# Late new-value products and split convolutions in a three-direction recurrent kernel

## The reference, cut to what matters

```python
gi = x @ wih.T ; gh = h @ whh.T            # three gates of 128 channels each
r = sigmoid(ir + hr) ; z = sigmoid(iz + hz)
n = tanh(i_n + r * h_n)
out = (1 - z) * n + z * h                  # the context, an output of the step
h = tanh(conv1d(out, cw) + cb)             # three taps along the line, 128 by 128 channels each
```

## Time and profile before

| | us |
|---|---|
| median of 3 runs | 370.1 (367.79 to 370.64) |
| the profiled execution | 367.54 |
| its span, first to last instruction | 365.8 |
| TensorE products, busy | 330.9 (90%) |
| VectorE busy | 309.7 (85%) |
| ScalarE busy | 277.8 (76%) |
| mean granted TensorE clock | 0.989 of full |

### The profile page before, as it was taken

The page is one execution under the profiler, slowest core; times in us unless marked ns, Lnnn a source line. Parts: engine busy times, 40 slices in busy tenths (PEclk is TensorE's granted clock), DMA queues, the critical chain, the costliest instruction groups (busy, mean ns, idle before and its releaser), DMA issues.

```text
span 365.8 us, 7776 instructions
## 1 busy us (share of the span) xinstructions
PE 330.9 (90%) x2720; PEld 260.7 (71%) x2720; DVE 309.7 (85%) x772; ACT 277.8 (76%) x590; POOL 4.2 (1%) x16
## 2 busy tenths in 40 slices
PE   1574758999998999999999999999999999999995
PEld 0233646778787888888888888888888888873442
DVE  2965778999997999889999999999998988887875
ACT  3977867888887888888888888888888888867400
POOL 2010000000000000000000000000000000000000
PEclk9988999999999999999999999999999999999999
DMA  8900000000000019100000000000000000000433
GB/s 301 372 1 2 2 0 2 0 2 3 0 3 0 2 26 398 39 0 0 0 0 0 0 0 0 0 0 0 0 0 0 0 0 0 0 0 34 174 139 115
DMA packets 5343, 14.75 MB, mean 40 GB/s; under 512 B 720, under 2 KB 848, under 8 KB 5328
## 3 DMA queue, kind: packets, MB, share of 16 engines
q1 hardware_dynamic: 5328, 14.55, 10.4%
HBM read 10.36 MB, written 4.19 MB: 40 GB/s over the span
## 4 chain that ended last, share of the span: by engine, by line
PE 75%; ACT 12%; issue 6%; DVE 5%; POOL 1%; POOLq 0%; ACTq 0%
PE rz_bank L765 19%; PE conv_bank L765 16%; PE rz_bank L768 9%; PE n_bank L765 9%; PE conv_bank L768 8%; PE n_bank L768 4%; ACT rz L440 3%; ACT x_col L435 2%; ACT x_rows L412 2%; DVE x_rows L571 1%; ACT hval L457 1%; ACT ctx_store L463 1%; PE rz_bank L851 1%; ACT nval L452 1%; DVE npre L657 1%
## 5 line engine op out<-in xcount | busy, mean ns | idle before, releaser
L765 PE MATMUL conv_bank<-ctx_store,w_parts 128*128 (+1 forms) x558 | 110.0, 277 | 6.5 <-ACT ctx_store L463 4.6
L765 PE MATMUL rz_bank<-h_parts,w_parts 128*128 128x256 f16 x372 | 76.1, 273 | 0.0
L440 ACT ACTIVATE rz<-rz_bank,descale 128x512 f32<-128x512 f32 x96 | 65.9, 687 | 10.4 <-PE rz_bank L765 5.6
L765 PEld LDWEIGHTS conv_bank<-ctx_store,w_parts 128*128 128x128 f16 x558 | 53.9, 98 | 25.2 <-ACT ctx_store L463 12.4
L452 ACT ACTIVATE nval<-npre 128x256 f32<-128x256 f32 x93 | 38.5, 413 | 41.5 <-DVE npre L669 41.5
L657 DVE SCALAR_TENSOR_TENSOR npre<-n_bank,descale,rz 128x256 f32<-128x256 f32 x93 | 44.9, 483 | 27.4 <-ACT rz L440 26.2
L768 PE MATMUL conv_bank<-ctx_store,w_parts 128*128 (+1 forms) x279 | 67.7, 276 | 0.0
L765 PE MATMUL rz_bank<-x_rows,w_parts 128*128 (+1 forms) x256 | 52.9, 274 | 4.5 <-DVE x_rows L571 4.5
L457 ACT ACTIVATE hval<-conv_bank,biases,descale 128x256 f32<-128x256 f32 x93 | 52.0, 560 | 3.1 <-PE conv_bank L765 3.0
L768 PE MATMUL rz_bank<-h_parts,w_parts 128*128 128x256 f16 x186 | 45.7, 273 | 0.0
L765 PE MATMUL n_bank<-h_parts,w_parts 128*128 128x256 f16 x186 | 45.7, 273 | 0.0
(11 more groups left out here) (118 smaller groups left out, 499.9 us busy)
## 6 DMA issues: line engine op xcount, KB each, us to landing
x<-x_dram SPq DMA_DIRECT2D x16, 512.0 KB, 7.8
out_dram<-x_rows SPq DMA_DIRECT2D x16, 256.0 KB, 2.0
ctx_store<-weights_dram SPq DMA_DIRECT2D x3, 576.0 KB, 11.7
ctx_store<-weights_dram SPq DMA_DIRECT2D x1, 192.0 KB, 12.6
biases<-biases_dram SPq DMA_DIRECT2D x1, 2.0 KB, 12.3
```

What stands on the lines that cost most here:

```text
L440: nc.scalar.activation(rz[k][:].rearrange("p g c -> p (g c)"), rz_bank[k][:], ACT.Sigmoid, scale=gate_scale(k)).then_inc(sig_done[k], 1)
L765: last = nc.tensor.matmul(out, w_block(HI, k, n), parts(hi_or_lo), start=start, stop=stop and hi_or_lo == LO, skip_group_check=True)
```

## The change: what it does

- **New-value products late.** The hidden part of the new value is written to the first half of `n_bank` (`hidden_new`, three products). `reset_hidden` multiplies it by the reset gate in place in PSUM. The three input products are then added onto it (`new_products`), in the block of `now`. `tanh_argument` is gone: the tanh reads PSUM with its scale in every step.
- **Convolutions in two parts.** `convolution_hi` (six products of the high context half) runs one block after the context, the first three of them ahead of `new_products` and three behind. `convolution_lo` (three products) runs in the next block, between the hidden gate products and `hidden_new`.
- **High context half on VectorE** (`context_hi`, now a one-source instruction), right behind `blend`. ScalarE's hidden tanh moves behind the sigmoid and the splits.
- **Head.** The strip of the last columns is two wide and is split before the first sigmoid, as are the weights "in 2"; the column piece between it and the next strip is split in block (1, 1). TensorE waits for the strip at block (0, 0). The six last warming products are gone.
- **Block (31, 2).** The first chunk parts are ahead of all else in it; the chunk parts after the blocks stand behind the late new-value products of the last step.

The diff, cut to its core:

```diff
-FRONT_WARM, CHAIN_WARM, LAST_WARM = 12, 4, 6
+FRONT_WARM, CHAIN_WARM = 12, 4
+CONV_AHEAD = 3
-LAST_COLS = Cells((2, H - 2), (W - 4, W))
+LAST_COLS = Cells((2, H - 2), (W - 2, W))
...
-    (0, 0): LAST_COLS,
-    (1, 0): Cells((2, 4), (0, W - 4)),
-    (1, 1): Cells((H - 4, H - 2), (0, W - 4)),
+    (1, 0): (Cells((2, 4), (0, W - 2)),),
+    (1, 1): (Cells((H - 4, H - 2), (0, W - 2)), Cells((4, H - 4), (W - 4, W - 2))),
...
-WAIT_SPLITS = ((0, 0), (1, 2), (2, 0), (3, 2), (4, 0), (7, 2), (8, 0), (10, 1))
+WAIT_SPLITS = ((0, 0), (0, 1), (1, 2), (2, 0), (3, 2), (4, 0), (7, 2), (8, 0), (10, 1))
...
@@ scalar
             weights_hi(UNITS.index("in 1"))
+            weights_hi(UNITS.index("in 2"))
+            x_hi(LAST_COLS, 2)
...
             def new_value(k, s):
-                if is_first(s):
...
-                else:
-                    act.wait_ge(npre_done[k], s)
-                    nc.scalar.activation(nval[k][:], npre[k][:], ACT.Tanh).then_inc(n_done[k], 1)
+                act.wait_ge(n_full[k], s + 1)
+                nc.scalar.activation(nval[k][:], n_bank[k][:, 0:COLS], ACT.Tanh,
+                                     scale=gate_scale(k)).then_inc(n_done[k], 1)
...
             def steps(t, j):
...
-                if exists(before[1], STEPS - 2) and not starting:
-                    hidden(*before)
                 if exists(nxt[1]):
                     gates(*nxt)
...
-                if exists(now[1]):
-                    context_hi(*now)
                 if exists(before[1], STEPS - 2):
-                    if starting:
-                        hidden(*before)
+                    hidden(*before)
                     hidden_hi(*before)
@@ vector
             weights_lo(UNITS.index("in 1"))
+            weights_lo(UNITS.index("in 2"))
+            x_lo(LAST_COLS)
...
             def reset_hidden(k, s):
                 dve.wait_ge(sig_done[k], s + 1)
-                dve.wait_ge(n_ready[k], s + 1)
-                nc.vector.scalar_tensor_tensor(npre[k][:], n_bank[k][:, COLS:2 * COLS], gate_scale(k),
-                                               rz[k][:, 0, :], ALU.mult, ALU.mult).then_inc(rh_done[k], 1)
+                dve.wait_ge(n_ready[k], s)
+                nc.vector.tensor_tensor(out=n_bank[k][:, 0:COLS], in0=n_bank[k][:, 0:COLS],
+                                        in1=rz[k][:, 0, :], op=ALU.mult).then_inc(rh_done[k], 1)
+
+            def context_hi(k, s):
+                dve.wait_ge(ctx_done[k], s + 1)
+                nc.vector.tensor_scalar(context_lines(k, s, HI), context[k][:].rearrange("p b l -> p (b l)"),
+                                        ACT_SCALE, None, ALU.mult).then_inc(ctx_hi_done[k], 1)
...
-            def tanh_argument(k, s):
...
             def steps(t, j):
...
                     blend(*now)
+                    context_hi(*now)
                 if exists(nxt[1]) and not is_first(nxt[1]):
                     reset_hidden(*nxt)
...
-                    tanh_argument(*nxt)
...
@@ tensor
-            warm(LAST_WARM)
...
+            def new_products(k, s):
+                first = is_first(s)
+                def x_parts(part):
+                    return x_line(k, s, part)
+                ahead(pe, s, x_parts(HI), x_parts(LO))
+                if not first:
+                    pe.wait_ge(rh_done[k], s)
+                passes(n_bank[k][:, 0:COLS], k, 2, x_parts, HI, start=first)
+                passes(n_bank[k][:, 0:COLS], k, 2, x_parts, LO, stop=True).then_inc(n_full[k], 1)
...
+            def hidden_new(k, s):
+                pe.wait_ge(n_done[k], s)
+                passes(n_bank[k][:, 0:COLS], k, GATES + 2, parts, HI, start=True)
+                passes(n_bank[k][:, 0:COLS], k, GATES + 2, parts, LO, stop=True) \
+                    .then_inc(n_ready[k], 1)
...
+            CONV_HI = [(tap, part) for tap in range(TAPS) for part in (HI, LO)]
+            def convolution_hi(k, s, first, end):
+                if first == 0:
+                    ahead(pe, s + 1, *(tap_lines(k, s, HI, tap) for tap in range(TAPS)))
+                    pe.wait_ge(ctx_hi_done[k], s + 1)
+                    if k == 2:
+                        pe.wait_ge(h_done[0], s + 1)
+                    elif not is_first(s):
+                        pe.wait_ge(h_done[1 if k == 1 else 2], s)
+                for tap, part in CONV_HI[first:end]:
+                    nc.tensor.matmul(out, w_block(part, k, 2 * GATES + tap), tap_lines(k, s, HI, tap), ...)
+            def convolution_lo(k, s):
+                ahead(pe, s + 1, *(tap_lines(k, s, LO, tap) for tap in range(TAPS)))
+                pe.wait_ge(ctx_lo_done[k], s + 1)
+                ...                                # three products, then conv_ready
...
             def steps(t, j):
+                # order: (chunk parts at (31, 2)), hidden_gates(now), convolution_lo(two back),
+                # hidden_new(now), wait for splits, input_gates(nxt), convolution_hi(one back, 0..3),
+                # new_products(now), convolution_hi(one back, 3..6)
...
-            pe.wait_ge(npre_done[1], STEPS - 1)
+            pe.wait_ge(n_done[1], STEPS)
             for c in (2, 3):
                 chunk_part(c, 0)
```

More of the change, by code:

```diff
@@ L472, in steps @@
                 now, nxt, before = lagged(t, j, 0), lagged(t, j, -1), lagged(t, j, 1)
[L474 removed]
                 if exists(now[1]):
[L476 removed]
+                    ahead(act, now[1], now[1] + 1)
                     new_value(*now)
[L478 to L479 removed]
                 if exists(nxt[1]):
@@ L816, in hidden_products, with tap_lines @@
                     .then_inc(n_ready[k], 1)
-            def convolution(k, s):
+            def tap_lines(k, s, part, tap):
+                return ctx_store[k][:, part, line(k, s), :, tap:tap + LINE]
+            CONV_HI = [(tap, part) for tap in range(TAPS) for part in (HI, LO)]
+            def convolution_hi(k, s, first, end):
                 out = conv_bank[k % 2][:, 0:COLS].rearrange("p (b l) -> p b l", b=B)
-                def tap_lines(part, tap):
-                    return ctx_store[k][:, part, line(k, s), :, tap:tap + LINE]
-                ahead(pe, s + 1, *(tap_lines(part, tap) for part in (HI, LO) for tap in range(TAPS)))
-                pe.wait_ge(ctx_hi_done[k], s + 1)
-                if k == 2:
-                    pe.wait_ge(h_done[0], s + 1)
-                elif not is_first(s):
-                    pe.wait_ge(h_done[1 if k == 1 else 2], s)
-                for part in (HI, LO):
-                    if part == LO:
-                        pe.wait_ge(ctx_lo_done[k], s + 1)
-                    for tap in range(TAPS):
-                        last = passes(out, k, 2 * GATES + tap,
-                                      lambda p: tap_lines(p, tap), part,
-                                      start=part == HI and tap == 0, stop=tap == TAPS - 1)
@@ new lines, in convolution_hi @@
+                if first == 0:
[6 more added lines that the diff above has]
+                for tap, part in CONV_HI[first:end]:
+                    nc.tensor.matmul(out, w_block(part, k, 2 * GATES + tap), tap_lines(k, s, HI, tap),
+                                     start=(tap, part) == (0, HI), stop=False, skip_group_check=True)
@@ new lines, in convolution_lo @@
+            def convolution_lo(k, s):
+                out = conv_bank[k % 2][:, 0:COLS].rearrange("p (b l) -> p b l", b=B)
+                ahead(pe, s + 1, *(tap_lines(k, s, LO, tap) for tap in range(TAPS)))
+                pe.wait_ge(ctx_lo_done[k], s + 1)
+                for tap in range(TAPS):
+                    last = nc.tensor.matmul(out, w_block(HI, k, 2 * GATES + tap), tap_lines(k, s, LO, tap),
+                                            start=False, stop=tap == TAPS - 1, skip_group_check=True)
@@ L873, in steps @@
             def steps(t, j):
-                k, s = lagged(t, j, 2)
-                if isinstance(s, int) and s == 0:
-                    pe.wait_ge(w_lo_done, UNITS.index(f"conv {k}") + 1)
-                if exists(s, STEPS - 2):
-                    convolution(k, s)
-                if j == 2 and isinstance(t, int) and t == STEPS - 1:
+                now, nxt, last, before = (lagged(t, j, lag) for lag in (0, -1, 1, 2))
+                if isinstance(t, int) and (t, j) == (STEPS - 1, 2):
                     pe.wait_ge(w_lo_done, len(UNITS))
-                    pe.wait_ge(npre_done[0], STEPS - 1)
+                    pe.wait_ge(n_done[0], STEPS)
                     pe.wait_ge(ctx_lo_done[0], STEPS)
```

127 lines of the change are left out of this document (60 added, 67 removed).

## The result

| | before | after |
|---|---|---|
| median, 9 runs each | 370.35 us (367.79 to 370.64) | 374.31 us (371.8 to 374.68) |
| the profiled execution | 367.54 | 373.17 |
| its span | 365.8 | 371.1 |

The changed kernel takes 1.011 times as long, interval 1.0077 to 1.0143. It is slower by about 4 us; 372.0 was forecast, with a range of 366.5 to 379. The runs of both kernels fall in two groups some 2.5 us apart (before three at 367.8 to 368.3 and six at 370.1 to 370.6, after two at 371.8 and 371.9 and seven at 373.2 to 374.7), and the profiled execution before (367.54) is like its lower ones, the one after like its upper ones.

The account below looks back on a forecast made before the run. The prediction took TensorE's own list of 27 products a block (2.96 us) to bound the loop from step 11; 2.6 + 0.8 - 1.4 + 1.3 = +3.3 gave 370.8 or 373.4, forecast 372 us, range 366.5 to 379.

Parts of the forecast that it names:

- Settled loop: From step 11 on: convolution 0.16 and reset 0.07 late behind the column copy, step 9.10 instead of 8.97, +2.6 us.
- Rival 1: Block behind the column copy: context high takes 0.44, step loses 0.37 rather than 0.23, time 376; chance 0.2.
- main case: Whole kernel: the prediction's own case, sum +3.3 us, from -1 to +5; chance 0.5.
- Opening: First blocks: products wait for the narrow strip, run at half clock, and the second tanh comes later; +0.8 us.
- split blocks: Steps 1 to 10: low split and low context leave the loop, the wait moves to the bank; -1.4 us.
- range for the clock: Opening: ends of its +0.8 us term, -1.2 (clock never low) and +1.5.
- End: After the last step: three late products behind sigmoid and reset stand ahead of eighteen output products; +1.3 us.
- sum +3.3: Whole kernel: the four terms added, 370.8 us from the profiled execution or 373.4 from the median.
- Rival 2: Split blocks fall to PE's floor if the bank wait is nothing: -7.4 instead of -1.4, time 366; chance 0.2.
- Rival 3: Looped part: address work on PE's queue shows at 0.05 to 0.1 us a block, time 377; chance 0.05.
- Rival 4: Whole kernel: nothing moves, PE's list being as long; only the end's +1.3 us; chance 0.05.

Follow-up runs that it names:

- e3: The changed kernel with the context's high half in a two-source form, at 442 instead of 302 ns; median 377.09 us, ratio to before 1.0229.
- e10: The changed kernel with direction 2's convolution in its own slot and the column copy in two halves; median 362.38 us, ratio to before 0.9817.
- e2: The changed kernel with twelve useless products in TensorE's 2.8 us wait ahead of block (1, 1)'s first convolution; median 372.63 us, ratio to before 1.0086.
- e9: The changed kernel with direction 2's convolution in the free half of its new-value bank, column copy whole; median 370.03 us, ratio to before 1.0022.
- e11: The changed kernel's loop with the head of the kernel before, six last warming products included; median 373.34 us, ratio to before 1.0119.
- e12: e10 with six chunk products moved ahead of the last late products in block (31, 2); median 362.07 us, ratio to before 0.981.
- e1: The changed kernel with the six last warming products put back; median 373.74 us, ratio to before 1.010.
- e8: The kernel before with only its column copy cut in two halves around the new-value tanh; median 366.56 us, ratio to before 0.9941.
- e6: The changed kernel with hidden tanh and hidden high half ahead of ScalarE's splits in the first blocks; median 385.92 us, ratio to before 1.0436.
- e7: The kernel before with the rebuilt head and nothing of the loop's rework; median 371.4 us, ratio to before 1.0037.

## Why the prediction was right, and where a step failed

- **Settled loop, +2.6, measured +2.5.** Step 9.092 against 9.10. Context high took 302 ns (taken 300), tanh out of PSUM 469 (461), reset in place 430 (taken 480, lower end 420). The chain copy, tanh, blend, context half, convolution was named link by link, and e3 shows it: the longer context half moved the step by its own length. That the sum came out so close is in part luck. It was 8.87 for the list plus 0.16 for the convolution and 0.07 for the reset; the runs have 8.903 for the list (e10) and 0.19 above it, all of it at the convolution, with no wait for the reset. The Trainium skill, "VectorE: DVE Perf Modes", section "Mode 2×_2P", has this one-source form take two elements a cycle, and the two-source form can't; 302 ns against 442 for the same 272 elements agrees.
- **What that step left out.** A second wait ends at the same place 0.09 earlier, the hidden tanh that frees the bank. The prediction had put that tanh at 1.44 to 2.00 of the block and never asked which convolution it releases there. In the settled loop it changed nothing in the forecast, and everything in what the cure is.
- **Rival 1, context half at 0.44.** Its price was 3.9 us over the main case; made so (e3), the ratio goes from 1.011 to 1.0229, some 4.4 us, and 28 steps at 0.143 make 4.0. The price of the mechanism was right and its condition was not met.
- **Opening and split blocks, +0.8 and -1.4, measured +1.4 together.** This is the term that was mis-sized, by 2.0 us in the profiled executions, and two misses partly cancel in it. The opening, up to the copy of step 1, came out at 0.0 (42.51 against 42.52) rather than +0.8, which is within the spread of the head. The split blocks, from there to the copy of step 11, came out at +1.4 rather than -1.4: step 1 to 2 lost 1.94, and steps 2 to 11 gained 0.54 (87.60 against 88.14). The prediction saw that the bank would take the place of the context half as the wait, and still gave these blocks a gain. Of the 1.94, 1.2 is the second fall of the clock (e2); of the rest, either the bank's wait away (e9, step 13.59) or the old head (e11, 13.56) takes nearly all. In steps 2 to 11 the bank's wait cost another 1.9: without it they take 85.69 (e9), a gain of 2.4 on the kernel before. The prediction's range for the clock, -1.2 to +1.5, was about the first fall only.
- **End, +1.3, measured +1.4.** Six of the eighteen products can be put into the pause, for 1.1 in the trace (e12).
- **From one execution to the median.** The sum +3.3 was set against a low profiled run, and the forecast put between its two answers (370.8 and 373.4). The second was the better one: the medians differ by 4.0, and 1.4 of the 2.3 us by which 372 missed comes from this choice. It bears on the term above too. In every trace with this loop and whole copies the settled step is 9.09 (but for e3's longer context half), and in four of them (the change, e1, e2, e11) steps 2 to 11 take 87.6, so what sets one execution apart from the next seems to lie ahead of the copy of step 2. An estimate from the medians, 4.0 less 2.5 and 1.4, leaves about +0.1 for opening and split blocks in a middling execution, not the +1.4 of the pair that was profiled; against the forecast -0.6 the miss is then 0.7.
- **Rival 2** (split blocks at the floor, 366) fails on the bank, as its condition said. With the bank's wait and the whole copy away the split blocks do give 4.9 of its 7.4 (e10 against e8). **Rival 3** (address work) is refuted by e10. **Rival 4**, the end's +1.3 alone, is refuted by the step.

## What to carry to other kernels

When an instruction is moved behind others on its queue, ask not only who reads its result but who waits for the buffer that it frees; here the hidden tanh did both, and its second role cost 1.9 us in steps 2 to 11 and hid what the change gains. Where two waits end within 0.1 us of each other at one place, removing either alone measures as nothing, which does not show that either is harmless: remove both. And a reordering on one engine has to be followed through the queues of those that work with it, as the 11.6 us of e6 show. Last, one profiled execution a kernel can come from either end of its spread: compare stretches that repeat between traces, and check the sum against the medians.

## What was not expected of the hardware

- **Whether the clock falls after a pause was not the pause's length alone.** It fell after TensorE's waits of 2.84 us (the changed kernel) and 2.52 (e7), and stayed at 1.00 after 2.99 (e3), 2.80 (e11) and 2.48 (before), all in the same step. One kernel may do both in different executions: with the longer context half three runs were at 376.0 to 376.7 and a mean clock of 0.982, three at 377.5 to 378.9 and 0.977, but only one of the first was profiled. The clock can't be the whole of such a gap: the kernel before has one of the same size, with mean clocks of 0.984 to 0.989 in its shorter runs and 0.981 to 0.986 in its longer ones. What decides either stays open. TensorE's order of time in the run with the longest of these waits, and its busy time by stretch right behind:

```profile
48.56 0.49 PE L834 MATMUL conv_bank<-ctx_store,w_parts 128*128 128x256 f16 x3 [2.99 <-ACT hval L453]
```

```profile
49.00:50.00 1.00, 1.00 (x12) 0.89 (x10) 0.75 (x3) 0.47 (x1) 0.00 (x0) 1.00 0.00 0
```

- **Full clock right ahead of the first products did not carry over.** In e1 six wide products ran from 23.72 at full clock; the granted clock was 0.90 in the microsecond in which they ended and 0.50 from 25 to 37 us, where narrower products and pauses follow.
- **The VectorE instruction that reads and writes PSUM in place** took 430 ns for 256 columns, beside 425 for one in SBUF and 483 for the form of the earlier trace rows that read PSUM with a scale and wrote SBUF.
- **A copy in two halves** is 2 x 638 ns against 1,085 for the whole: 0.19 us more of ScalarE's time a step, and still 0.6% (some 2 us) gained on the kernel before, since here it counts when the engine is held, not how long.
